# Attention loop of a graph layer: third query chunk ahead of the bias's last parts and of the next group's first index copy, and nine unused products per group instead of sixteen

## The reference

```python
Q, K, V = (h @ Wq + bq), (h @ Wk + bk), (h @ Wv + bv)       # 8 heads of 16
scores = sum(Q[dst] * K[src], per head) * scale + (edge_attr @ We + be)
scores = scores - segment_max(scores, dst)[dst]
probs = exp(scores) / (segment_sum(exp(scores), dst) + 1e-10)[dst]
x = x + segment_sum(probs * V[src], dst) @ Wo + bo           # layer 0: attention
h2 = logmap0(relu(layernorm(x))) @ W.T + b                   # layer 1: graph convolution
x = x + expmap0(segment_sum(h2[src] * dinv[src] * dinv[dst], dst))
```

## Time and profile before

| | |
|---|---|
| median of 3 runs | 928.81 us (926.0 to 931.78) |
| the profiled execution's own time | 929.15 us |
| its span, first to last instruction | 927.0 us |
| mean granted TensorE clock | 0.957 of full speed |
| PE busy | 816.5 us (88%), 5435 products |
| PE weight loads busy | 618.9 us (67%) |
| DVE busy | 696.5 us (75%) |
| ACT busy | 543.4 us (59%) |
| POOL busy | 575.7 us (62%) |
| L1819, the unused products | 137.8 us busy, 506 of them |
| chain that ended last | PE 56%, POOL 15%, issue 9%, DMA 7%, DVE 6%, ACT 4% |

### The profile page before, as it was taken

One profiled execution on the slowest core, in us unless ns is written; L12 is line 12 of the kernel. 1 busy time (PEld: TensorE's weight loads), 2 busy tenths in 40 slices (PEclk: granted clock), 3 DMA queues, 4 the chain that ended last, 5 costly groups with the idle time before them and its releaser, 6 DMA issues.

```text
span 927.0 us, 21469 instructions
## 1 busy us (share of the span) xinstructions
PE 816.5 (88%) x5435; PEld 618.9 (67%) x5435; DVE 696.5 (75%) x2543; ACT 543.4 (59%) x1392; POOL 575.7 (62%) x597
## 2 busy tenths in 40 slices
PE   5559988999999999999999999975699899989883
PEld 2236766677777777677777776764487777868673
DVE  9826766777777777777777877879998878878752
ACT  4486654666666666666666666517665555655530
POOL 0176766767777677777777777600476756676762
PEclk9868999999999999999999999997799999999996
DMA  6752455545544445444444444420322212222220
GB/s 177 210 139 86 123 109 114 133 110 127 131 119 131 114 121 137 116 118 132 114 122 134 115 121 127 119 68 26 103 61 62 66 54 68 54 71 57 68 58 27
DMA packets 103595, 95.99 MB, mean 104 GB/s; under 512 B 35964, under 2 KB 87393, under 8 KB 103553
## 3 DMA queue, kind: packets, MB, share of 16 engines
q0 software_dynamic: 25600, 66.10, 26.1%
q1 hardware_dynamic: 77961, 29.51, 12.7%
HBM read 84.40 MB, written 11.15 MB: 103 GB/s over the span
## 4 chain that ended last, share of the span: by engine, by line
PE 56%; POOL 15%; issue 9%; DMA 7%; DVE 6%; ACT 4%; SPq 1%; POOLq 0%; DVEq 0%
POOL kv L853 15%; PE ps_s L1819 13%; PE ps_q L1842 11%; PE ps_r L1862 10%; PE ps_f L1897 6%; DMA kv<-hs_tab,idx 5%; PE ps_c L1811 4%; PE ps_s L1829 4%; ACT ST L1611 3%; PE ps_f L1921 1%; PE ps_f L1920 1%; PE ps_c L1807 1%; DMA qwin<-q_tab 1%; PE ps_c L1870 1%; PE ps_f L2033 1%
## 5 line engine op out<-in xcount | busy, mean ns | idle before, releaser
L814 POOL DMA_INDIRECT kv<-kv_tab,idx x416 | 405.2, 974 | 194.1 <-issue 119.6
L853 POOL DMA_INDIRECT kv<-hs_tab,idx x176 | 170.2, 967 | 140.9 <-DMA hs_tab<-qkv 55.7
L1611 ACT ACTIVATE ST<-ps_s,imj 128x512 f32<-128x512 f32 (+1 forms) x128 | 77.1, 602 | 140.3 <-PE ps_s L1829 140.2
L1819 PE MATMUL ps_s<-rep_hi,iota_b 128*128 128x512 bf16 x506 | 137.8, 389 | 0.0
L1842 PE MATMUL ps_q<-qwin,ST 128*128 128x128 f32 x832 | 126.2, 292 | 8.0 <-DMA qwin<-q_tab 4.5
L1842 PEld LDWEIGHTS ps_q<-qwin,ST 128*128 128x128 f32 x832 | 108.7, 197 | 22.2 <-issue 17.8
L1594 ACT ACTIVATE S<-iota,nloc 128x128 f32<-128x128 f32 x384 | 122.0, 388 | 0.0
L1082 DVE TENSOR_TENSOR prod<-kv,ps_q 128x512 f32<-128x512 f32 (+1 forms) x128 | 71.6, 575 | 53.6 <-PE ps_q L1842 51.4
L1862 PE MATMUL ps_r<-wv,S 128*128 128x137 f32 x832 | 110.8, 286 | 0.0
L1862 PEld LDWEIGHTS ps_r<-wv,S 128*128 128x128 f32 x832 | 103.2, 192 | 7.7 <-issue 6.8
L2022 PE MATMUL ps_r<-qkv,xt 128*128 128x128 f32 x800 | 92.3, 276 | 0.8 <-ACT xt L1737 0.8
(11 more groups left out here) (279 smaller groups left out, 1381.5 us busy)
## 6 DMA issues: line engine op xcount, KB each, us to landing
kv<-kv_tab,idx POOLq DMA_INDIRECT x416, 2.7
attr_s<-in_attr SPq DMA_DIRECT2D x32, 192.0 KB
kv<-hs_tab,idx POOLq DMA_INDIRECT x176
kv_tab<-qkv SPq DMA_DIRECT2D x4, 640.0 KB, 3.4
x_tab<-x SPq DMA_DIRECT2D x32, 64.5 KB, 2.1
qwin<-q_tab SPq DMA_DIRECT2D x32, 64.0 KB
xwin<-in_x SPq DMA_DIRECT2D x32, 64.0 KB
xwin<-x_tab SPq DMA_DIRECT2D x32, 64.0 KB
```

Of the source, the lines that this page charges most:

```text
L814: pool.indirect_dma_start(out=kv[:, b, t, :], out_offset=None, in_=kv_tab, in_offset=bass.IndirectOffsetOnAxis(ap=idx[:, b, t:t + 1], axis ...
L853: pool.indirect_dma_start(out=kv[:, j, t, 0:D], out_offset=None, in_=hs_tab, in_offset=bass.IndirectOffsetOnAxis(ap=idx[:, j, t:t + 1], ax ...
L1611: A.activation(ST[:, b, t0:t1, :], row_index(c), ACT.Abs, bias=imj[:, 0:1], scale=-1.0).then_inc(s_sta, 1)
L1819: M.matmul(ps_s[1][:], iota_b[:], busy_cols, start=True, stop=True)
```

## The change

Three things change in PE's step, and with them the start.

1. `bias(g, b, (2, 3))` and index copy 0 of group g+1 stood at the end of the step before; now they stand behind the third query chunk of group g. So index copies 0 and 1 of group g+1 now follow each other directly.
2. `BUSY` goes from (3, 4, 3, 3, 3) to (0, 1, 2, 3, 3): none ahead of the third query chunk, one ahead of L1891, two between the counting and L1902.
3. At the start PE does two bias parts instead of four and no index copy of group 1; ACT no longer makes chunk 0 of group 1's `ST` between its two copies but in the first step, behind the twelve one-hot tiles. Nothing of the result changes.

```diff
-BUSY = (3, 4, 3, 3, 3)
+BUSY = (0, 1, 2, 3, 3)
...
-            def step(g, b, nodes=True, more=True, far=True, rows=(0, 1, 2, 3)):
+            def step(g, b, nodes=True, more=True, far=True):
                 if more:
-                    row_one_hots(g + 1, 1 - b, rows)
+                    row_one_hots(g + 1, 1 - b, range(NCH))
...
                 forward_copies()
-                row_one_hots(1, 1, (0,))
                 backward_copies()
                 act.wait_ge(s_nloc, 1)
                 one_hots(0, 0, (0, 1, 2))
-                step(0, 0, nodes=False, rows=(1, 2, 3))
+                step(0, 0, nodes=False)
...
-            def step(g, b, edges=True, nodes=True, more=True, far=True):
+            def step(g, b, edges=True, nodes=True, more=True):
                 if edges:
-                    stay_busy(BUSY[0])
                     query(g, b, (2,))
+                    bias(g, b, (2, 3))
                 if edges and more:
-                    spread_rows(g + 1, 1 - b, (1,))
+                    spread_rows(g + 1, 1 - b, (0, 1))
                 if edges:
                     query(g, b, (3,))
...
-                if edges and more:
-                    bias(g + 1, 1 - b, (2, 3))
-                if edges and more and far:
-                    spread_rows(g + 2, b, (0,))
...
                 spread_rows(0, 0, (0, 1, 2, 3))
-                bias(0, 0, (0, 1, 2, 3))
+                bias(0, 0, (0, 1))
                 query(0, 0, (0, 1))
-                spread_rows(1, 1, (0,))
                 pe.wait_ge(s_oh, 2)
                 step(0, 0, nodes=False)
                 step(1, 1)
                 with pe.Fori(1, GROUPS // 2 - 1) as n:
                     step(2 * n, 0)
                     step(2 * n + 1, 1)
-                step(GROUPS - 2, 0, far=False)
+                step(GROUPS - 2, 0)
                 step(GROUPS - 1, 1, more=False)
                 step(GROUPS, 0, edges=False)
```

## The result

The changed kernel took 989.85 us (median of 4 runs, 986.23 to 990.96), the kernel before 927.4 us beside it (923.36 to 931.78). The ratio is 1.067, with a 95% interval of 1.061 to 1.072: slower by about 62 us, outside the predicted range.

What follows compares the result with a forecast made beforehand. PE's waits and products on the path were taken to bound the lap. Gains of 7.5 (loop), 2 (start), 1.8 (loads) and 0.9 (end), less 2.4 (clock), made 9.8 us: 919.0 us forecast, range 909 to 931.

Steps and rivals of the forecast that it cites:

- the clock term: PE's granted clock in the loop: two falls at 1.2 us each, 2.4 us lost.
- the clock falls (slower): Rival: PE idles between third query chunk and window sums, clock falls; 953 us at one fall a group; chance 0.13.
- The sum of one lap: One group in the loop: 0.87 - 0.54 - 0.08, so 0.25 us gained, a lap of 16.93.
- The 0.08: Third query chunk on PE: deduction because a chunk beginning after a wait is dearer, 1.07 against 0.98 us.
- The head start of the chunk: Third query chunk starts 1.16 us earlier, but the two index copies standing together use that up.
- Removed products: Unused products on PE: 0.22 us each; the seven removed are worth at most 1.5 us a lap.
- Start: Before the loop: three fewer unused products and moved copies gain 2 us, bounds 0 to 3.
- Late loads: Two steps where PE waits for the queries' window: each wait 0.9 us shorter, 1.8 us gained.
- End: Last step, which has no index copies: keeps the 0.87, so 0.9 us gained.
- POOL: POOL's 13 gathers a lap, with slow ones, take 16.6 to 16.9 us, keeping up with a lap of 16.93.
- The wait does not reach the path: Rival: the 0.54 us delay of the window sums vanishes; 898 us, or 903 to 907 if POOL-bound; chance 0.10.

Runs made afterwards that it cites:

- bias_between: Changed kernel with bias parts 2 and 3 between index copies 0 and 1 instead of ahead of copy 0; 967.79 us, ratio 1.037.
- fill_waits: Changed kernel plus five unused products a group: three between index copies 0 and 1, two ahead of index copy 2; 919.95 us, ratio 0.981.
- fill_only: Kernel before with nothing moved, only its unused products cut to (0, 1, 2, 3, 3); 905.98 us, ratio 0.968.
- copy_first: Changed kernel with index copy 0 back ahead of the third query chunk and the bias parts behind the chunk; 903.88 us, ratio 0.969.
- filler_back: Changed kernel's order with unused products (0, 4, 3, 3, 3), so only the three ahead of the third query chunk stay away; 1021.83 us, ratio 1.090.
- no_fill: Kernel before with its order kept and no unused products at all; 1024.69 us, ratio 1.104.
- head_fill: Kernel before with its order kept and only the three unused products ahead of the third query chunk removed; 920.95 us, ratio 0.991.
- first_wait: Changed kernel plus only three unused products a group between index copies 0 and 1; 919.45 us, ratio 0.986.
- second_wait: Changed kernel plus only two unused products a group ahead of index copy 2; 947.01 us, ratio 1.017.

## Why the prediction was wrong

**The step that failed is the clock term**: "I take two falls in the loop, 2.4". Both factors of the term were too small. The changed kernel fell in 23 of the 24 laps counted, and in 30 of all 31, not in two. A fallen lap is 19.44 - 16.93 = 2.5 us longer, not 1.2. Over 30 laps that is about 75 us, against 989.85 - 919.95 = 70 measured by filling the waits. The rival "the clock falls (slower)" named the place and the mechanism, and at one fall a group gave 953; it had a chance of 0.13. Two things misled me. I judged the stretch by its longest single idle time against 1.60 and 2.38 us at two falls, where bias_between fell with none over 0.43. And I priced a fall by the earlier trace rows, in which only part of the 26 sums, from 615.65 to 620.2, ran at the low clock. The stretch behind that of the earlier trace rows is mostly at full:

```profile
618.00:620.00 2.00, 2.00 (x17) 2.00 (x17) 0.46 (x3) 0.00 (x0) 0.00 (x0) 0.89 0.12 33
```

A fall just ahead of the window sums, as in the lap of 413.73, costs nearly all of them.

**The sum of one lap was right.** At full clock I had a lap of 16.93; fill_waits has 16.93 over 24 laps, with the changed order and the changed fillers elsewhere. Its mean starts over these laps, counted from the last turn back: third query chunk 5.17 (I had 5.11), index copy 1 7.79 (7.72), index copy 2 9.02 (8.96), L1894 13.64 (13.57). The 0.08 that I took off for a chunk behind a wait was misread: no wait stands ahead of the chunk at 306.83, and the third chunk takes 1.00 us in the changed order (339.68 to 340.68 in fill_waits). A loss of that size is there all the same, 0.06 of it already ahead of the chunk; its source was not looked for. The head start of the chunk was used up by the adjacent copies, and the gain came from the fillers ahead of L1890 and L1901, as stated.

**Removed products.** 0.22 us each holds: copy 0 and the three fillers behind it in fill_waits start 0.30 apart and the fillers' row is 0.82 long, as before.

**Start.** I took 2 us. L1890 came first at 67.78, where L1891 came at 69.77: 2.0 us. It did not last in the changed kernel, whose first lap took 21.36 us at a mean clock of 0.61 against 15.82 before.

**Late loads.** I took 1.8 us gained. In fill_waits PE waited 2.12 us for the queries' window once instead of twice, but the clock fell behind it and its fourth lap took 26.17. Laps 4 and 5 are 43.1 us there and 41.7 before, while two ordinary laps are 0.5 shorter: 1.9 lost, not gained. The wrong step is that I took the shorter wait for the whole cost.

**End.** 0.9 us: the last lap is 15.21 in fill_waits and 16.09 before. Right.

**POOL.** I had it keep up with 16.6 to 16.9. Its bound is the bare 16.25, as fill_only shows. It did not bind in the changed kernel, where POOL waited 47.0 us in 17 times for L1890 alone.

**"The wait does not reach the path".** Wrong, as I had it: index copy 2 and the window sums stood later in the lap in every kernel with adjacent copies. But its 26 us could be had in two other ways: by an order with the copies apart (copy_first), and with no step moved at all (fill_only).

Two things stay open. filler_back and no_fill both settle at 20.49 us a lap though they have different work and different clocks (means 0.83 and 0.67); why they agree was not tried. And the lap of 25 to 27 us behind a late load, in fill_waits, fill_only, head_fill and copy_first, was seen but not taken apart.

## What to carry to other kernels

In this kernel an unused product that fills a wait cost nothing, and one on the path cost up to its 0.22 us. Remove the second kind only as far as the clock holds (with all sixteen gone it fell in every lap), keep the first, and when steps are moved, move the fillers to where the new waits are. Try the two halves of a change apart: here the fewer fillers alone gave 0.968, and the moves with them 1.067. Before pricing a change in PE's order by microseconds of waiting, look at how much PE does in the thin stretch ahead of its longest burst, and at the granted clock behind it; a fall of the clock cost here ten times what the change could gain. A step that another engine must read before the next can go (index copy 0) belongs ahead of independent work, not behind it.

## What the runs showed of the hardware that was not expected

- The granted clock fell in all of 24 laps with no recorded idle time on PE over 0.43 us in the stretch before (bias_between), and held in 24 of 24 with five products more in a stretch that was not shorter (fill_waits, 4.18 us from 339.68 to 343.86, against 3.81).
- A fallen lap was 1.6 us longer in first_wait (18.50 at a mean clock of 0.91, against 16.93) and 2.9 to 3.3 in five laps of second_wait (19.85 to 20.27 at 0.83, against 16.96). The time at the low level was not the same each time.
- Once the clock falls in every lap, the laps are very even: 20.44 to 20.53 us in filler_back from the eighth to the 28th.
- POOL's gathers go on at 1.25 us each without a pause over whole laps: 82 or 83 in 103 us (fill_only, copy_first).
